# A reordered end of a loop, four copies and a root on VectorE, and an early table load, in a two-stage attention kernel

## Chip, cores and metric

One Trainium2 chip, one of its cores. The metric is the device time of one execution in microseconds (us). The kernel is written at the level of instructions: each engine has its own program, and semaphores order the engines among each other.

## What is computed

A batch of 32 sequences of 256 tokens with 256 features. A first attention with 16 heads, over batch 0 alone, is added to `x`. Then each batch goes through this, with `input_features` = `ctx` and `query_feature` = `x`:

```
norm_X   = layernorm(input_features, norm1)
norm_F_L = layernorm(query_feature, norm2)
attended = softmax(norm_F_L @ norm_X.T / 16) @ norm_X
h        = gelu(attended @ fc1_w.T + fc1_b)          # 4 hidden values per token
cross    = h @ fc2_w.T + fc2_b
nc       = layernorm(cross, norm3)
self     = softmax(nc @ nc.T / 16) @ nc
out      = norm_F_L + gamma2 * (cross + gamma1 * self)
```

Because `cross` is a linear function of 4 hidden values and a constant, the kernel never builds it at 256 features. The second attention works on rows of 6 values per token (`u`, `uK`); its layernorm needs one value per token, the variance (a quadratic form of `h`), and its reciprocal square root (`r3`).

## The kernel before

After a prologue (the first attention), the work falls into two loops.

**First loop**, 32 steps `b`, one for each batch (L1242 on TensorE, L900 on ScalarE, L540 on VectorE). `score` (L1078) makes the scores in one of three PSUM banks, `maximum` on VectorE their row maxima, `exponentials` on ScalarE the weights, `weights_turned` (L1089) turns them on TensorE, `weights_copied` on ScalarE copies them out of PSUM. Every four batches, a quad: `project` and `project_back` make values (`turned_values` and `values` copy them), `apply` and `apply_back` multiply weights and values (`applied` and `saved` copy them). The hidden values of the quads go through Gelu in three shares: `hidden(0)` at b = 21 (quads 0 to 3), `hidden(1)` at b = 29 (quads 4 and 5), `hidden(2)` in the second loop (quads 6 and 7). Gelu and Exp need different tables of ScalarE, so a Gelu among Exps costs two table loads.

**Second loop**, steps `p` = 0 to 20, one pair of batches in each of the first 16. For a pair: `turn` (L1140) turns its small rows (the operands of the scores) into PSUM bank 4, `turned` (L890, ScalarE) copies them out as `sT`, `scores` (L1162) makes the scores, `maxima` (L577, VectorE) their row maxima, `maxima_turn` (L1178) turns those into bank 5, `maxima_turned` (L923, ScalarE) copies them out as `nm2T`, `shift` (L1187) adds them to the scores, `weights` (L929, ScalarE) takes Exp. Every second step `attend` (L1198) multiplies weights and values of a quad into bank 5, `collected` copies them out as `o2T` (the tile's storage is named wqT, and so is it in the trace), `back` turns them, `returned` (VectorE) divides, `output_cuts` (GpSimd) splits into bf16 parts `sC`, `output_turn` and `output_turned` turn them, and `output` makes the result, which `finish` (L593, VectorE) adds to `Fall`, from where SyncE stores it.

Step `p` of TensorE is: `maxima_turn(p)`, `scores(p+1)`, `turn(p+2)`, `shift(p)`, then `output(p-5)`, and `attend` with `output_turn` at even p, `back` at odd p. `keep_busy(n, bank)` (L967) is n matmuls whose result nobody reads; each is two instructions in the trace.

**The algebra of shares 1 and 2** (16 tiles each) is made by GpSimd: `squares` (L744), `scaled` (L750, which ends with the power -1/2 of the variances, L758, and with `u`, L759), `keyed` (L762) and `right` (L767). VectorE then makes the left operands in `second_left` (L452, six instructions). GpSimd's order is `right(0)`, `squares(0)`, `scaled(0)`, `keyed(0)`, `right(1)`, `squares(1)`, `output_cuts(0)`, `scaled(1)`, `output_cuts(1)`, `keyed(1)`, `right(2)`, `output_cuts(2..7)`. The results of `scaled(1)`, `keyed(1)` and `right(2)` are needed by VectorE at p = 8 and by TensorE at p = 10; `output_cuts(q)` is needed by TensorE at p = 2q + 4. `newton` (L438) is one step of a reciprocal square root on VectorE, three instructions; share 0 uses it in the first loop already.

Of the kernel before, what the change touches and what calls it, by code (L numbers as in the profile page):

```python
# [72 lines left out]
def build(nc, x, ctx, x0t, c0t, wqt, wkt, wvt, params, out):  # L73
# [38 lines left out]
    minus_half = sb("minus_half", [P, 16])  # L112
    XT = sb("XT", [P, 4, DC, 2 * N])
# [127 lines left out]
    STORED = tuple(range(PAIRS))  # L241

# [50 lines left out]
    def _(dve):  # L293
# [158 lines left out]
        def second_left(h):  # L452
            G = quarter(h)
            dve.wait_ge(summed_ok, 8 * (h + 1))
            dve.wait_ge(rooted_ok, 7 * (h + 1))
# [127 lines left out]

        def returned(q):
# [18 lines left out]
        saved(QUADS - 1)  # L603
        for p in range(2 * QUADS + 5):
            if p + 1 < PAIRS:
                maxima(p + 1)
            if p % 2 == 1 and 3 <= p < 2 * QUADS + 1:
                returned((p - 3) // 2)
# [4 lines left out]
            if p == 0:  # L613
                hidden_input(2)
            if p == 2:
                second_left(0)
            if p == 8:
                second_left(1)

    @block.gpsimd  # L620
    def _(pool):
# [128 lines left out]
        def scaled(h):  # L750
# [7 lines left out]
            rooted(pool.tensor_tensor(y, var[:, G], minus_half[:, 0:GROUP // 2], ALU.pow))  # L758
# [38 lines left out]
        squares(0)  # L797
        scaled(0)
# [12 lines left out]
    def _(act):  # L811
# [88 lines left out]
        for b in range(B):  # L900
# [5 lines left out]
            if b >= 1:  # L906
                weights_copied(b - 1)
            exponentials(b)
            if b % 4 == 1 and q >= 1:
# [13 lines left out]
        def maxima_turned(p):  # L923
# [3 lines left out]
            act.activation(nm2T[:, p % 2, :], bank[5][0:2 * VW, 0:P // 2].bitcast(BF16), ACT.Copy).then_inc(m_ok, 1)  # L927
# [39 lines left out]
    def _(pe):  # L967
# [210 lines left out]
        def maxima_turn(p):  # L1178
            pe.wait_ge(max2_ok, p + 1)
            if p >= 3 and p % 2 == 1:  # L1180
# [3 lines left out]
            pe.transpose(bank[5][0:2 * VW, 0:P // 2].bitcast(BF16), nm2[:, p % 2, :, :].rearrange("p m r -> p (m r)"),  # L1184
# [57 lines left out]
        for b in range(B + 1):  # L1242
# [3 lines left out]
            if b < B:  # L1246
# [10 lines left out]
            if b == 31:  # L1257
                scores(0)
# [14 lines left out]
            if b == 31:  # L1273
                turn(1)
        for p in range(2 * QUADS + 5):
            if p < PAIRS:
                maxima_turn(p)
            if p == 0:
                keep_busy(3, 6)
                apply(QUADS - 1)  # L1280
# [4 lines left out]
            if p + 2 < PAIRS:  # L1285
                turn(p + 2)
            if p < PAIRS:
# [70 lines left out]
```

## Time and profile before

| | us |
|---|---|
| median of 3 runs | 236.84 (236.83 to 241.5) |
| the profiled execution | 236.88 |
| its span, first to last instruction | 234.8 |
| share of the span: TensorE (PE), VectorE (DVE), ScalarE (ACT), GpSimd (POOL) | 89%, 78%, 66%, 62% |
| second loop, from its first maxima turn to the end of the span | 171.2 to 234.8 |

All times in rows are microseconds from the start of the span, unless marked ns. PE is TensorE's matmul and PEld its weight load. The page adds up how long each engine was busy and cuts the span into 40 slices. The timeline lists instructions by start and duration, with the idle time in front of them and what ended it. The chain of work that ended last is followed back from the last instruction, each piece to what released it.

### The profile page before, as it was taken

To read this page: it belongs to the slowest core of one execution; us is meant where nothing else is said; L and a number is where in the kernel's file an instruction comes from. 1 tells how busy PE (TensorE), PEld (TensorE's weight loads), DVE (VectorE), ACT (ScalarE), POOL (GpSimd) and SP (SyncE) were. 2 spreads that over 40 slices of the span, in tenths; PEclk is the share of its full clock that TensorE was granted. 3 is DMA by queue.
4 is the path that set the end of the run, shared out by engine and by line. 5 is a ranking of instruction groups with operands and counts; after the bars stand their busy time and mean duration, and the time that the engine had idled before them with its cause. 6 is when DMAs were issued, how large, how long until landed. Compare 5 with 4: busy or idle time off the path is not lost.

```text
span 234.8 us, 4965 instructions
## 1 busy us (share of the span) xinstructions
PE 209.6 (89%) x1730; PEld 151.6 (65%) x1730; DVE 182.5 (78%) x360; ACT 153.8 (66%) x295; POOL 146.7 (62%) x240
## 2 busy tenths in 40 slices
PE   8999979987779999999999989997998898899760
PEld 8776646776556978789787867794766444454230
DVE  6499977779979988878778999993333867988673
ACT  2177865544546877778777896789558786677520
POOL 6536551467499999987987793934953288322320
PEclk9999999999999999999999999999999999999855
DMA  6990000084540554426535200000000004444458
GB/s 227 384 332 4 1 1 3 0 223 138 178 179 3 179 179 138 149 78 180 179 108 158 94 3 0 6 0 1 3 0 0 3 15 167 179 181 180 183 212 324
DMA packets 14712, 26.81 MB, mean 114 GB/s; under 512 B 1760, under 2 KB 1760, under 8 KB 14688
## 3 DMA queue, kind: packets, MB, share of 16 engines
q1 hardware_dynamic: 14400, 25.98, 32.3%
q10 hardware_dynamic: 288, 0.52, 0.7%
q8 instruction: 14, 0.23, 0.4%
q14 instruction: 10, 0.08, 0.1%
HBM read 18.11 MB, written 8.39 MB: 113 GB/s over the span
## 4 chain that ended last, share of the span: by engine, by line
PE 53%; DVE 20%; ACT 10%; POOL 8%; issue 6%; DVEq 0%; ACTq 0%; POOLq 0%
PE psum L1085 15%; PE psum L1022 9%; PE psum L1093 5%; DVE xN L381 4%; DVE bn L361 4%; PE psum L970 3%; PE psum L1123 3%; DVE Fall L596 2%; DVE hmax L399 2%; PE psum L1105 2%; PE psum L1205 2%; DVE nmax L523 2%; ACT L862 2%; PE psum L1238 1%; ACT E L887 1%
## 5 line engine op out<-in xcount | busy, mean ns | idle before, releaser
L1085 PE MATMUL psum<-XT,Fall 128*128 128x256 f32 x256 | 61.0, 381 | 1.7 <-ACT Fall L857 1.7
L1085 PEld LDWEIGHTS psum<-XT,Fall 128*128 128x128 f32 x256 | 46.1, 190 | 7.3 <-ACT Fall L857 2.3
L700 POOL TENSOR_SCALAR cN<-cN,nmean,rstd 128x256 f32<-128x256 f32 x64 | 37.4, 594 | 2.5 <-POOL rstd L687 2.1
L680 POOL TENSOR_TENSOR xN<-xN,tgt 128x512 f32<-128x512 f32 x28 | 35.6, 1277 | 4.8 <-DVE xN L381 4.8
L687 POOL TENSOR_TENSOR rstd<-vps,minus_half 128x8 f32<-128x8 f32 (+1 forms) x16 | 24.2, 1512 | 19.9 <-DVE vps L372 19.6
L887 ACT ACTIVATE E<-psum,nmax 128x256 f32<-128x256 f32 x64 | 26.8, 474 | 11.9 <-DVE nmax L523 11.9
L880 ACT ACTIVATE PT<-psum 128x512 f32<-128x512 f32 x32 | 19.1, 598 | 22.7 <-PE psum L1093 22.6
L523 DVE TENSOR_REDUCE nmax<-psum 128x2 f32<-128x512 f32 x32 | 22.0, 687 | 14.7 <-PE psum L1085 14.2
L381 DVE TENSOR_SCALAR xN<-xN,bn,rstd 128x256 f32<-128x256 f32 x64 | 32.8, 558 | 0.5 <-POOL rstd L687 0.4
L581 DVE TENSOR_REDUCE nm<-psum 128x4 bf16<-128x1024 f32 x16 | 19.5, 1220 | 8.2 <-PE psum L1173 8.2
L854 ACT ACTIVATE XT<-psum,b1s,w1s 128x512 f32<-128x512 f32 x32 | 23.0, 795 | 4.0 <-PE psum L1022 4.0
L857 ACT ACTIVATE Fall<-psum,par 128x512 f32<-128x512 f32 x32 | 23.4, 794 | 2.8 <-PE psum L1022 2.8
L361 DVE BATCH_NORM_STATS2 bn<-xN 128x6 f32<-128x512 f32 x32 | 21.9, 690 | 2.1 <-POOL xN L680 2.1
L361 DVE BATCH_NORM_STATS2 bn<-cN 128x6 f32<-128x512 f32 x32 | 22.2, 695 | 0.1
L1093 PE MATMUL psum<-ident,E 128*128 128x128 f32 x128 | 20.1, 280 | 1.3 <-ACT E L887 1.3
L1093 PEld LDWEIGHTS psum<-ident,E 128*128 128x128 f32 x128 | 14.4, 141 | 9.1 <-issue 6.3
L596 DVE TENSOR_TENSOR Fall<-psum,Fall 128x1024 f32<-128x1024 f32 x15 | 18.1, 1216 | 0.8 <-PE psum L1238 0.8
L1022 PE MATMUL psum<-ident,cN 128*128 128x128 f32 x128 | 17.4, 275 | 1.2 <-POOL cN L700 1.2
L970 PE MATMUL psum<-meanw 128*128 128x128 f32 x116 | 17.5, 301 | 1.0 <-POOL meanw L622 1.0
L1022 PE MATMUL psum<-ident,xN 128*128 128x128 f32 x128 | 16.9, 274 | 1.3 <-DVE xN L381 1.1
L935 ACT ACTIVATE PT<-psum 128x1024 f32<-128x1024 f32 x16 | 16.3, 1019 | 1.0 <-PE psum L1192 1.0
L970 PEld LDWEIGHTS psum<-meanw 128*128 128x128 f32 x116 | 15.6, 211 | 1.7 <-POOL meanw L622 1.0
(173 smaller groups left out, 351.9 us busy)
## 6 DMA issues: line engine op xcount, KB each, us to landing
cN<-ctx SPq DMA_DIRECT2D x32, 256.0 KB, 3.0
xN<-x SPq DMA_DIRECT2D x32, 256.0 KB, 4.1
out<-Fall SPq DMA_DIRECT2D x32, 256.0 KB, 2.3
x0T<-x0t ACTq DMA_DIRECT2D x1, 256.0 KB, 3.0
c0T<-c0t ACTq DMA_DIRECT2D x1, 256.0 KB, 3.9
wqT<-wqt SPq DMA_DIRECT2D x1, 256.0 KB, 3.6
wkT<-wkt SPq DMA_DIRECT2D x1, 256.0 KB, 4.1
wvT<-wvt SPq DMA_DIRECT2D x1, 256.0 KB, 4.8
```

The lines of the kernel that those rows point to most:

```text
L361: dve.bn_stats(bn[:, (b // 2) % 4, side, b % 2, :], src[:, b % SLOTS, :].rearrange("p (t d) -> p d t", t=NT)).then_inc(st_ok, 1)
L381: dve.tensor_scalar(own, own, stat(p, 1, m, t, 1), root_of(p, 1, m, t), ALU.subtract, ALU.mult)\
L523: dve.tensor_reduce(nmax[:, b % 2, :], tiles(bank[SBANK1[b % 3]]), AX.X, ALU.max, negate=True)\
L680: pool.tensor_tensor(xN[:, b % SLOTS, :], xN[:, b % SLOTS, :], tgt2[:, :, :].rearrange("p t d -> p (t d)"), ALU.add).then_inc(y_ok, 1)
L687: pool.tensor_tensor(rstd[:, p % 4, sides, :].rearrange("p s k -> p (s k)"), vps[:, p % 4, sides, :].rearrange("p s k -> p (s k)"), minus_ ...
L700: pool.tensor_scalar(own, own, nmean[:, p % 4, NT * m + t:NT * m + t + 1], root_of(p, 0, m, t), ALU.add, ALU.mult)\
L857: act.activation(Fall[:, 2 * p:2 * p + 2, c, :], tiles(own), ACT.Identity, bias=c_("b2", c), scale=c_("w2", c)).then_inc(evac_ok, 1)
L887: act.activation(E[:, b % 2, t * N:(t + 1) * N], bank[SBANK1[b % 3]][:, t * N:(t + 1) * N], ACT.Exp, bias=nmax[:, b % 2, t:t + 1]).then_in ...
L970: pe.matmul(bank[b][:, 0:P], meanw[:, :], meanw[:, :], start=True, stop=True)
L1022: last = pe.transpose(bank[TBANK[n % 3]][:, m * N + t * P:m * N + (t + 1) * P], z[:, (2 * p + m) % SLOTS, t * D + c * P:t * D + (c + 1) * ...
L1085: last = pe.matmul(bank[SBANK1[b % 3]][:, t * N:(t + 1) * N], Fall[:, b, c, t * P:(t + 1) * P], XT[:, p % 4, c, m * N:(m + 1) * N], start= ...
L1093: last = pe.transpose(bank[SBANK1[b % 3]][:, k * N + t * P:k * N + (t + 1) * P], E[:, b % 2, t * N + k * P:t * N + (k + 1) * P], ident[:, :])
```

## The change

It does the following; nothing else in the program differs.

1. End of the first loop. On ScalarE `turned_values(7)` goes ahead of `exponentials(29)` and `weights_copied(29)` and `(30)` go behind the exponentials of their step. On TensorE `score(31)` moves from the front of step 31 to step 30, and `scores(0)` behind `weights_turned(30)`.
2. Start of the second loop. On TensorE at p = 0, `scores(1)` and `shift(0)` go ahead of `apply(7)`, `apply_back(7)` goes to p = 1, and the fillers change from 3 + 5 + 13 to 2 + 13 + 4 calls. On ScalarE `weights(0)` goes ahead of `applied(7)`, and on VectorE `saved(7)` behind `maxima(1)` and `turned(2)`. The turned maxima of p = 3 go to bank 7, not bank 5.
3. `turned(2)` to `turned(5)` are made by VectorE.
4. `hidden(2)` (Gelu) goes behind `weights(1)`, and an Exp of one column (`warm`) follows it, so that Exp's table is loaded there.
5. For share 2, GpSimd makes the variances right behind `squares(1)`, VectorE the root (`second_root`, behind step 3: two integer instructions and three Newton steps, 11 instructions in all that each wait for the one before), and GpSimd goes on with `u`. `right(2)` comes ahead of `output_cuts(1)`.

```diff
+        def turned(p):                                   # VectorE
+            dve.wait_ge(st_mm, p + 1)
+            dve.wait_ge(s2_mm, p - 1)
+            dve.tensor_copy(sT[:, p % 2, :], bank[4][:, 0:NT * P].bitcast(BF16)).then_inc(sT_ok[p % 2], 1)
+        def second_root():
+            G = quarter(1)
+            v, y = var[:, G], r3[:, G]
+            dve.wait_ge(rooted_ok, 12)
+            link(dve.tensor_scalar(y.bitcast(I32), v.bitcast(I32), 1, None, ALU.logical_shift_right))
+            link(dve.tensor_scalar(y.bitcast(I32), y.bitcast(I32), -1.0, RSQRT_SEED, ALU.mult, ALU.add))
+            for _ in range(NEWTON - 1):
+                newton(v, y, t3[:, G])
+            newton(v, y, t3[:, G])
...
         maxima(0)
-        saved(QUADS - 1)
         for p in range(2 * QUADS + 5):
             if p + 1 < PAIRS:
                 maxima(p + 1)
+            if p < 4:
+                turned(p + 2)
...
             if p == 0:
+                saved(QUADS - 1)
                 hidden_input(2)
             if p == 2:
                 second_left(0)
+            if p == 3:
+                second_root()
...
         squares(1)                                       # GpSimd
+        variances(1)
         output_cuts(0)
         scaled(1)
+        right(2)
         output_cuts(1)
         keyed(1)
-        right(2)
...
-            if b >= 1:                                   # ScalarE, first loop
+            if 1 <= b < B - 2:
                 weights_copied(b - 1)
+            if b == B - 3:
+                turned_values(QUADS - 1)
             exponentials(b)
...
+            if b >= B - 2:
+                weights_copied(b - 1)
...
             if p == 0:                                   # ScalarE, second loop
+                weights(0)
                 applied(QUADS - 1)
+            if 4 <= p < PAIRS - 2:
+                turned(p + 2)
+            if 1 <= p < PAIRS:
+                weights(p)
             if p == 1:
                 hidden(2)
-            if p + 2 < PAIRS:
-                turned(p + 2)
-            if p < PAIRS:
-                weights(p)
+                act.activation(warm[:, :], minus_half[:, 0:1], ACT.Exp)
...
-            if b < B:                                    # TensorE, first loop
+            if b < B - 1:
                 score(b)
...
-            if b == 31:
-                scores(0)
+            if b == B - 2:
+                score(B - 1)
...
+            if p == 1:                                   # TensorE, second loop
+                apply_back(QUADS - 1)
             if p + 1 < PAIRS:
                 scores(p + 1)
             if p == 0:
-                apply_back(QUADS - 1)
...
+                shift(0)
+                apply(QUADS - 1)
+                turn(2)
+                keep_busy(2, 5)
...
+                    if p == 2:
+                        keep_busy(4, 6)
```

## Rows read from the trace of the kernel before

**Rows 1.** The page: busy time by engine, and TensorE's granted clock in 40 slices.
```profile
PE 209.6 (89%) x1730; PEld 151.6 (65%) x1730; DVE 182.5 (78%) x360; ACT 153.8 (66%) x295; POOL 146.7 (62%) x240
...
PEclk9999999999999999999999999999999999999855
```

**Rows 2.** Timeline, TensorE at the join: start, duration, engine, line, tiles, count, idle before.
```profile
164.00 0.44 PE L1113 MATMUL psum<-ident,vT 128*128 128x128 f32 x2 [1.22 <-ACT vT L868]
164.37 1.05 PE L1123 MATMUL psum<-PT,V 128*5 128x256 f32 x16
...
166.07 1.95 PE L1085 MATMUL psum<-XT,Fall 128*128 128x256 f32 x8
...
170.58 0.66 PE L1093 MATMUL psum<-ident,E 128*128 128x128 f32 x4 [0.25 <-ACT E L887]
...
177.14 3.17 PE L970 MATMUL psum<-meanw 128*128 128x128 f32 x26
180.23 0.24 PE L1184 MATMUL psum<-identb,nm 128*64 128x128 bf16 x1
```

**Rows 3.** Timeline, ScalarE: table loads of the last two Gelus.
```profile
161.54 1.28 ACT L887 ACT_TABLE_LOAD   x1
...
176.55 1.28 ACT L862 ACT_TABLE_LOAD   x1
...
178.61 1.28 ACT L935 ACT_TABLE_LOAD   x1
```

**Rows 4.** Timeline, VectorE early in the second loop: its idle time.
```profile
174.24 0.20 DVE L538 COPY OA<-psum 128x40 f32<-128x40 f32 x1 [4.26 <-PE psum L1131]
...
181.50 1.23 DVE L581 TENSOR_REDUCE nm<-psum 128x4 bf16<-128x1024 f32 x1 [3.62 <-PE psum L1173]
...
184.44 1.22 DVE L581 TENSOR_REDUCE nm<-psum 128x4 bf16<-128x1024 f32 x1
```

**Rows 5.** Timeline, GpSimd: squares of share 2, first and last instruction.
```profile
178.18 1.00 POOL L738 TENSOR_TENSOR kv<-ha,Q 128x400 f32<-128x400 f32 x1 [4.50 <-ACT ha L862]
...
180.26 0.41 POOL L748 TENSOR_TENSOR W<-kv 128x80 f32<-128x80 f32 x1
```

**Rows 6.** Chain that ended last, in order of time: start, duration, what.
```profile
182.64 0.26 DVE uK L456
...
189.56 2.93 POOL r L758
...
201.26 0.41 PE psum L1224 x4
```

**Rows 7.** Timeline, TensorE in the second loop: maxima turns (L1184) and an output turn.
```profile
189.05 0.22 PE L1184 MATMUL psum<-identb,nm 128*64 128x128 bf16 x1 [0.34 <-ACT wqT L942]
...
194.74 0.40 PE L1224 MATMUL psum<-identb,sC 128*128 128x128 bf16 x4 [0.67 <-POOL sC L794]
...
210.26 0.22 PE L1184 MATMUL psum<-identb,nm 128*64 128x128 bf16 x1
...
213.36 0.22 PE L1184 MATMUL psum<-identb,nm 128*64 128x128 bf16 x1 [0.26 <-ACT wqT L942]
...
215.90 0.22 PE L1184 MATMUL psum<-identb,nm 128*64 128x128 bf16 x1
```

**Rows 8.** Groups by line and form, VectorE: busy us, mean ns, idle before.
```profile
L405 DVE COPY PT<-psum 128x512 f32<-128x512 f32 x8 | 5.5, 683 | 0.8 <-PE psum L1051 0.8
L348 DVE TENSOR_SCALAR kv<-psum,par 128x256 f32<-128x256 f32 x4 | 1.7, 478 | 1.5 <-PE psum L990 1.5
L440 DVE SCALAR_TENSOR_TENSOR t<-t,var 128x32 f32<-128x32 f32 x3 | 0.8, 278 | 0.1
L439 DVE TENSOR_TENSOR t<-r 128x32 f32<-128x32 f32 x3 | 0.6, 191 | 0.1
```

**Rows 9.** Timeline, TensorE: the same attend (L1205) at either clock.
```profile
217.36 1.05 PE L1205 MATMUL psum<-PT,u 128*6 128x256 f32 x16
...
221.29 1.43 PE L1205 MATMUL psum<-PT,u 128*6 128x256 f32 x16 [0.63 <-DVE co L590]
```

**Rows 10.** Windows: length, busy us of PE, PEld, DVE, ACT, POOL, then PEclk, DMA, GB/s.
```profile
222.00:224.00 2.00, 2.00 (x18) 0.88 (x10) 0.35 (x2) 0.38 (x1) 0.79 (x3) 0.50 0.47 171
```

More of the change, by code:

```diff
@@ L241, in build, with maxima_bank @@
     STORED = tuple(range(PAIRS))
+    def maxima_bank(p):
+        return bank[7 if p == 3 else 5][0:2 * VW, 0:P // 2].bitcast(BF16)
     def result(n):
@@ L582, in maxima @@
                               ALU.max, negate=True).then_inc(max2_ok, 1)
+        def turned(p):
[11 more added lines that the diff above has]
+            newton(v, y, t3[:, G])
+            ALG["root"] = count[0]
         def returned(q):
@@ L748, in squares, with variances @@
             summed(pool.tensor_tensor(W5[:, G, :].unsqueeze(3), q[:, :, :, 0:1], q[:, :, :, 4:5], ALU.add))
-        def scaled(h):
+        def variances(h):
             G = quarter(h)
@@ L757, in scaled @@
             rooted(pool.tensor_scalar(var[:, G], var[:, G], EPS, None, ALU.add))
-            rooted(pool.tensor_tensor(y, var[:, G], minus_half[:, 0:GROUP // 2], ALU.pow))
+            if h == 0:
+                rooted(pool.tensor_tensor(y, var[:, G], minus_half[:, 0:PART], ALU.pow))
+        def scaled(h):
+            G = quarter(h)
+            y = r3[:, G]
+            if h == 1:
+                pool.wait_ge(alg, ALG["root"])
             rooted(pool.tensor_tensor(u[:, G, 0:H + 1], ha[:, G, :], y.unsqueeze(2).to_broadcast([P, GROUP // 2, H + 1]),
@@ L797, in _ @@
         squares(0)
+        variances(0)
         scaled(0)
@@ L926, in maxima_turned @@
                 act.wait_ge(s2m_mm, p - 1)
-            act.activation(nm2T[:, p % 2, :], bank[5][0:2 * VW, 0:P // 2].bitcast(BF16), ACT.Copy).then_inc(m_ok, 1)
+            act.activation(nm2T[:, p % 2, :], maxima_bank(p), ACT.Copy).then_inc(m_ok, 1)
         def weights(p):
@@ L1179, in maxima_turn @@
             pe.wait_ge(max2_ok, p + 1)
-            if p >= 3 and p % 2 == 1:
+            if p == 3:
+                pe.wait_ge(o_saved, QUADS)
+            elif p >= 3 and p % 2 == 1:
                 pe.wait_ge(o2T_ok, (p - 1) // 2)
@@ L1183, in maxima_turn @@
                 pe.wait_ge(co_ok, (p - 2) // 2)
-            pe.transpose(bank[5][0:2 * VW, 0:P // 2].bitcast(BF16), nm2[:, p % 2, :, :].rearrange("p m r -> p (m r)"),
+            pe.transpose(maxima_bank(p), nm2[:, p % 2, :, :].rearrange("p m r -> p (m r)"),
                          identb[:, :]).then_inc(m_mm, 1)
@@ L1272, in _ @@
                 turn(0)
-            if b == 31:
+            if b == B - 1:
+                scores(0)
                 turn(1)
@@ L1283, in _ @@
             if p == 0:
-                apply_back(QUADS - 1)
-            if p + 2 < PAIRS:
-                turn(p + 2)
-            if p < PAIRS:
-                shift(p)
-                if p < 2:
-                    keep_busy((5, 13)[p], 5)
+                shift(0)
+                apply(QUADS - 1)
+                turn(2)
+                keep_busy(2, 5)
+            else:
+                if p + 2 < PAIRS:
+                    turn(p + 2)
+                if p < PAIRS:
+                    shift(p)
+                    if p == 1:
+                        keep_busy(13, 5)
             if p == 2 * QUADS:
```

9 lines of the change are left out of this document (4 added, 5 removed).

## The prediction

> **What bounds the kernel now.** I read the page first: TensorE is busy 89% of the span and was granted full clock until the last slices [rows 1]. A share of busy time says little for the second loop, since fillers are in it, so I went on to the timelines of all engines from 157 us on, and then to the chain that ended last. Three stretches show.
>
> The join of the loops, 164 to 180 us: TensorE waits 1.22 us for the copy of the last values and once more ahead of the last turned weights [rows 2]. ScalarE loads Exp's table in front of that copy, and later pays two loads one behind the other around the third Gelu [rows 3], during which TensorE runs a filler of 26 instructions, 3.17 us [rows 2]. VectorE is idle for 4.26 and 3.62 us [rows 4].
>
> The middle, 182 to 204 us: the chain goes from VectorE (182.64) through GpSimd, with its power of 2.93 us, to the output turn at 201.26 on TensorE [rows 6]. The reader is to see that GpSimd, idle before, is late with `sC` twice, by 0.67 us [rows 7] and about as much at 201.26.
>
> The steady part: from 210.26 to 213.36 an even step takes 3.10 us, from there to 215.90 an odd one 2.54 [rows 7], a pair 5.64. VectorE needs, in a pair, two maxima and two sums of about 1.13 us pitch and a division of 0.35, so 4.9 us. It has 0.75 us to spare, not more.
>
> **The change, step by step.** I write out the new order with the durations of the rows. Each start stands beside the old one.
>
> *End of the first loop.* The copy of the last values no longer stands behind the table load, so TensorE's wait of 1.22 us goes. `score(30)` ends at 162.62 as before; from start to start `project_back` takes 0.37 (164.00 to 164.37), `apply(6)` 0.98, a `score` 1.78 of its 1.95 [rows 2], so `score(31)` is through at 165.75. `turned(0)` on ScalarE begins at 166.95 (behind `weights_copied(29)`) and `exponentials(31)` behind it, 167.45 to 168.28. TensorE's last filler there ends at 169.25, so the last weights are turned at 169.3, not 170.58 [rows 2]: 1.3 us earlier. ScalarE then copies two weights and the operand of pair 1, until 171.0; `scores(1)` goes at 171.1, `shift(0)` at 171.4, `apply(7)` to 172.7. `turn(2)` and a filler of 0.55 end at 173.5: maxima turn 1. The filler of 26 follows `shift(1)` at 174.9 and ends at 178.0: **maxima turn 2 at 178.0, old 180.23** [rows 2], 2.2 us earlier.
>
> *Gelu and its loads.* They now lie behind `weights(1)`: ScalarE ends that at 176.05, load 1.28, Gelu 0.26, load 1.28, the short Exp 0.2, free at 179.1. The first load is under the filler. The second is not quite: `shift(2)` could go at 178.6 and waits until 179.4, 0.8 us. Then `attend(0)` and the filler of 8: maxima turn 3 at 181.6. A rule speaks against this edit. The row shows a load of 1.28 us with the Gelu or Exp beginning 0.02 us behind it [rows 3]. "ScalarE: Activation LUTs" of the Trainium skill, section "What ACT_TABLE_LOAD costs", counts a drain of about 1.38 us on top, about 2.66 us a switch; the trace doesn't agree, and by that rule the sum below would lose about 1.3 us more and end at 236.6.
>
> *Copies on VectorE.* No row shows a bf16 copy of 128x512 from PSUM on VectorE. The same count in f32 takes 683 ns, half of it 478 [rows 8]; I take 0.68 (0.6 pitch) as the nearest in elements, with 0.48 as the lower bound and ScalarE's own 0.60 between. The first two are hidden in VectorE's idle time [rows 4]; `turned(4)` and `turned(5)` lie on its path. "VectorE: DVE Perf Modes" of the Trainium skill, in its section on the TRN2 errata, gives (120 + elements/acceleration) cycles at 0.96 GHz for a PSUM source, an estimate of 0.66 us at one element a cycle and 0.39 at two; no run here shows this form, and at 0.39 the sum would be some 0.5 us lower.
>
> *VectorE from 179.8 on.* `maxima(3)` ends at 179.8, `turned(4)` 0.6, `second_left(0)` 1.8 (182.64 to 184.44 [rows 4, 6]): 182.2. `scores(4)` ends at 182.2 as well, so `maxima(4)` ends at 183.4, `turned(5)` at 184.0, `returned(0)` 184.4. Here comes the root: 11 instructions with a wait each. The rows of the same code in the first loop are 191 and 278 ns for 32 columns [rows 8], the larger mean containing a disturbed one, and 0.22 us from start to start. I take 0.22, so 2.45 us; at 0.30 it is 3.3, and nothing smaller than 0.2 is in sight: 2.2. GpSimd's squares and variances are ready for it: squares took 178.18 to 180.67 [rows 5], now 177.7 to 180.2, and five small instructions more end at 181.9, while the root begins at 184.3. So this wait costs nothing; its cover is 2.4 us. The root ends at 186.8. Behind it on VectorE's queue stands `maxima(5)`, whose scores are ready at 185.4: it ends at 188.0, and with it comes **maxima turn 5 at 188.2, old 189.05** [rows 7]. Of the 2.2 us gained at the join, 0.85 is left: VectorE takes back the rest.
>
> *GpSimd afterwards.* The division of quad 0 is ready at 184.4; cuts(0) take 1.7 us, `u` then waits for the root only to 186.8, `right(2)` ends near 189.5, cuts(1) run 190.8 to 192.5, `keyed(1)` ends by 195.6. TensorE asks for cuts(1) at 193.2, so the wait of 0.67 us [rows 7] goes, and the one at 201.26 [rows 6] too. Steps 5 to 7 last 2.54 + 3.10 + 2.54 rather than 189.05 to 197.94: maxima turn 7 at 193.9, the back turn of quad 2 at 195.4, VectorE's division at 195.85, old 197.35: **1.5 us earlier**. From there VectorE is busy without a gap (finish, maxima, finish, `second_left(1)` of 1.8, maxima), as it was before, so of the second GpSimd wait nothing more can be had: the sum for that pair is 4.9 + 1.8 = 6.7 us against TensorE's 5.64. The 1.5 us pass through to the end, since steps 10 to 15 and the tail are the same.
>
> *The sum.* +2.2 (join) − 1.35 (VectorE in steps 2 to 5) + 0.7 (GpSimd's lateness) = 1.55 us, rounded 1.5. Against the profiled execution, 236.88 with 234.8 of span, that is 235.3 with a span of 233.2; the median, 236.84, is the same within 0.04. With the copy at 0.48 and the root at 2.2 it is 0.5 less, 234.8; with the root at 3.3 it is 0.85 more, 236.2. A difference within 2% (4.7 us) is about what a measurement of this kernel can tell from no change.
>
> **Rivals.**
> 1. *VectorE's root undoes all.* If each of the 11 instructions takes 0.30 us, or GpSimd's variances come behind 184.3 because Gelu is late, `maxima(5)` ends near 188.9 and maxima turn 5 is where it was; what is left is the 0.7 of GpSimd: 236.2. For it: the 278 ns row. Against it: the smaller tile, and 2.4 us of cover.
> 2. *More is had.* VectorE's copies are short, the `shift(2)` wait is nil because `maxima_turned(2)` finds ScalarE free, and the two `sC` waits with the `cT` waits behind them give their full 1.9 us: 2.2 + 1.9 − 0.5 of VectorE = 3.6 us, 233.3. Against it: VectorE has no gap from p = 7 to p = 9.
> 3. *Slower: the clock falls in the second loop.* Fillers go from 21 to 19 calls and other places; in my order TensorE idles 1.1 us ahead of `scores(1)`, 0.5 at 178.9, 0.9 at 183.2 and 0.9 ahead of maxima turn 5. In the trace the clock is full from the start until the tail, where at 222 us it is 0.50 [rows 10], 1.2 GHz, behind two gaps of 0.3 and 0.6 us and little work. There an attend takes 1.43 us rather than 1.05 although it began before the fall was complete [rows 9], and copies of four instructions grow by half. A pair of steps would be some 2.5 us longer, so from about 3.5 us of steps at the low clock on it is slower than before; two pairs give 235.3 + 5 = 240.3, one 237.8. Against it: in the old trace TensorE idled 1.22, 0.6 and 0.67 us in this region at full clock [rows 2, 7].
> 4. *No effect.* The join's gain is eaten in steps 2 to 5 and second-order waits (bank 7 of p = 3 behind `saved(7)`, `cT`) take the rest: 236.9.
>
> **How the numbers follow.** Forecast 0.50 (its own range 234.6 to 236.0), root dear 0.17 (236.2), more 0.15 (233.3, of which under 232.1 0.03), no effect 0.11 (236.9), clock 0.07 (237.8 to 240.3, above 241.6 0.01 or so). The likeliest gives 235.3. The range leaves out the clock case and the outer part of "more": 233.5 to 236.9. Faster by over 2% 0.03, within 2% 0.95, slower 0.02.
>
> **What would show it.** In the changed kernel's trace: Right for the join if the last turned weights begin near 169.3 and maxima turn 2 near 178.0; the table load behind Gelu should stand ahead of the short Exp, and `weights(2)` have none. Right for VectorE if the copies last about 0.68 us, the root 2.45, and maxima turn 5 stands near 188.2 with its wait on VectorE. Right for GpSimd if no output turn waits for `sC`. Wrong if VectorE waits for GpSimd ahead of the root, if the clock row shows less than full before slice 37, if the division of quad 2 doesn't stand 1.5 us earlier than 197.35, or if steps 10 to 15 have another length than before.

## The result

The changed kernel takes 232.99 us (median of 4 runs; 232.56 to 233.31) against 236.84, a ratio of 0.984 with a 95% interval of 0.982 to 0.986: 3.85 us less, where 1.5 were forecast, and below the range of 233.5 to 236.9. Some runs of a kernel are slower than the rest, at a lower granted clock, and the ratios leave them out (here the one of 241.5 us). The profiled execution took 233.31 with a span of 231.5.

The page of the changed kernel, busy time and granted clock in 40 slices:

```profile
PE 206.6 (89%) x1726; PEld 150.5 (65%) x1726; DVE 186.3 (80%) x375; ACT 151.8 (66%) x292; POOL 143.9 (62%) x239
...
PEclk9999999999999999999999999999999999999995
```

Beside [rows 1] VectorE works 3.8 us more in a span that is 3.3 us shorter, and the clock is low in one slice, not in three.

The timeline of TensorE in the changed kernel (start, duration, line, tiles, count, idle before and its releaser). L1226 is the maxima turn:

```profile
168.67 0.60 PE L1133 MATMUL psum<-ident,E 128*128 128x128 f32 x4
...
170.45 0.39 PE L1213 MATMUL psum<-sT 36*128 36x256 bf16 x4 [1.00 <-ACT sT L928]
...
177.52 0.24 PE L1226 MATMUL psum<-identb,nm 128*64 128x128 bf16 x1
...
178.85 0.39 PE L1234 MATMUL psum<-nm2T,sel 2*128 2x256 bf16 x4 [0.43 <-ACT nm2T L965]
...
183.52 0.94 PE L1010 MATMUL psum<-meanw 128*128 128x128 f32 x6 [0.69 <-DVE sT L592]
...
187.34 0.24 PE L1226 MATMUL psum<-identb,nm 128*64 128x128 bf16 x1 [0.43 <-DVE nm L586]
...
192.31 0.40 PE L1266 MATMUL psum<-identb,sC 128*128 128x128 bf16 x4
...
202.20 0.22 PE L1226 MATMUL psum<-identb,nm 128*64 128x128 bf16 x1 [0.85 <-DVE co L611]
...
213.48 0.22 PE L1226 MATMUL psum<-identb,nm 128*64 128x128 bf16 x1
```

The last turned weights begin at 168.67, not 170.58 [rows 2]; maxima turn 2 at 177.52, not 180.23; maxima turn 5 (187.34) waits 0.43 us for VectorE and stands 1.7 us ahead of the old 189.05 [rows 7]; the output turn at 192.31 no longer waits for GpSimd, where 0.67 us went before; turn 10 waits 0.85 us for VectorE's division.

The same execution on ScalarE, VectorE and GpSimd (three timelines):

```profile
177.14 1.28 ACT L1000 ACT_TABLE_LOAD   x1
178.44 0.20 ACT L1000 ACTIVATE warm<-minus_half 128x1 f32<-128x1 f32 x1
178.54 0.25 ACT L965 ACTIVATE nm2T<-psum 64x128 bf16<-64x128 bf16 x1
```
```profile
183.05 0.41 DVE L592 COPY sT<-psum 128x512 bf16<-128x512 bf16 x1
...
183.73 0.16 DVE L598 TENSOR_SCALAR r<-var 128x16 int32<-128x16 int32 x1
...
185.85 0.18 DVE L445 SCALAR_TENSOR_TENSOR r<-t,r 128x16 f32<-128x16 f32 x1
186.06 1.22 DVE L586 TENSOR_REDUCE nm<-psum 128x4 bf16<-128x1024 f32 x1
```
```profile
181.13 0.26 POOL L782 TENSOR_SCALAR var<-var 128x16 f32<-128x16 f32 x1
...
183.94 0.33 POOL L819 CAST sC<-co 128x160 bf16<-128x160 f32 x1 [2.55 <-DVE co L611]
...
186.10 0.32 POOL L791 TENSOR_TENSOR u<-ha,r 128x80 f32<-128x80 f32 x1 [0.32 <-DVE r L445]
```

The load is where it was meant to be: the Exp of one column begins 0.02 us behind it, and `nm2T` is copied right after. A copy lasts 0.41 us, the root 183.73 to 186.03, 2.3 us, with `maxima(5)` behind it. GpSimd has the variances at 181.39 and then idles 2.55 us: in this gap the power of 2.93 [rows 6] would nearly have fitted.

### Where the time went

Lengths between landmarks, in us, each worked out from the starts of the maxima turns in a kernel's timeline; `mt0` is maxima turn 0, "end" that of the last sum, and the stretch from `mt15` to it is called the tail. "q" is the length of the same eight matmuls of the q projection, some 5 us into the span. The kernels of the other rows are explained under Experiments.

| trace | q | mt0 at | mt0-mt2 | mt2-mt5 | mt5-mt9 | mt9-mt15 | mt15-end |
|---|---|---|---|---|---|---|---|
| before | 2.71 | 171.17 | 9.06 | 8.82 | 12.53 | 17.42 | 11.98 |
| after | 2.40 | 169.20 | 8.32 | 9.82 | 11.40 | 17.83 | 11.15 |
| join_alone | 2.75 | 169.73 | 8.32 | 8.82 | 12.53 | 19.95 | 12.02 |
| gpsimd_alone | 1.99 | 170.31 | 9.07 | 8.82 | 11.38 | 17.83 | 11.15 |
| join_gpsimd | 2.88 | 169.87 | 8.32 | 8.82 | 11.37 | 17.85 | 12.05 |
| copies_act | 2.15 | 168.94 | 8.33 | 9.65 | 11.40 | 17.84 | 11.15 |
| root_gpsimd | 1.99 | 168.53 | 8.32 | 9.73 | 11.37 | 17.84 | 11.14 |
| plain_best | 2.43 | 169.41 | 8.31 | 9.26 | 11.73 | 17.85 | 11.14 |
| no_warm | 2.74 | 169.71 | 8.32 | 9.44 | 11.27 | 18.11 | 11.14 |

From before to after: 1.97 to mt0, 0.74 to mt2, −1.00 to mt5, 1.13 to mt9, −0.41 to mt15, 0.83 in the tail, together 3.26 us, the difference of the spans (3.3).

The medians differ by 3.85, about half a microsecond more. Half of that is that the profiled run of the changed kernel lies 0.32 above its median. The other half lies outside the spans: what a run takes beyond its span is 1.8 to 1.9 us in every run of the kernels that have the Newton steps on VectorE (the changed kernel among them), 1.9 to 2.0 in root_gpsimd, and 2.1 to 2.2 in all others, before among them. So some 0.3 us of the gain goes with the root's move to VectorE, though no trace shows where.

### The profile page after: what moved, and what is told of

It is laid out like the page before. It is cut to its first block, busy times and chain, and to the rows that moved or that the text cites. A ratio compares the mean times of both kernels' runs of the same rounds, so it can differ in the third digit from the quotient of the medians.

```text
span 231.5 us, 4967 instructions
## 1 busy us (share of the span) xinstructions
PE 206.6 (89%) x1726; PEld 150.5 (65%) x1726; DVE 186.3 (80%) x375; ACT 151.8 (66%) x292; POOL 143.9 (62%) x239
## 3 DMA queue, kind: packets, MB, share of 16 engines
HBM read 18.11 MB, written 8.39 MB: 114 GB/s over the span
## 4 chain that ended last, share of the span: by engine, by line
PE 61%; DVE 21%; ACT 8%; issue 5%; POOL 2%; DVEq 0%; ACTq 0%; POOLq 0%
PE psum L1125 18%; PE psum L1062 10%; PE psum L1133 5%; PE psum L1010 4%; DVE Fall L617 4%; DVE xN L385 3%; DVE bn L365 3%; PE psum L1163 3%; PE psum L1247 3%; PE psum L1145 3%; DVE hmax L403 2%; DVE nmax L528 2%; PE psum L1280 2%; PE psum L1213 2%; PE psum L1234 2%
## 5 line engine op out<-in xcount | busy, mean ns | idle before, releaser
L1010 PE MATMUL psum<-meanw 128*128 128x128 f32 x112 | 17.0, 302 | 1.7 <-POOL meanw L647 1.0
L1010 PEld LDWEIGHTS psum<-meanw 128*128 128x128 f32 x112 | 15.1, 212 | 2.5 <-POOL meanw L647 1.0
```

Source lines behind the costliest of these rows:

```text
L1010: pe.matmul(bank[b][:, 0:P], meanw[:, :], meanw[:, :], start=True, stop=True)
```

## Experiments

Each is a small edit of the changed kernel unless it says otherwise. Times are medians with the lowest and highest of all runs. The groups of experiments ran on different chips, and mt0 moves with the prologue by up to 1.1 us between executions, so a difference of a few tenths between two medians says little. The lengths from mt0 to mt15 repeat within 0.03 us where the clock is full (47.37, 47.38 and 47.37 in three profiles of the changed kernel, 47.83 twice in before), and the argument rests on them.

### The parts alone

**join_alone** keeps items 1 and 2 and undoes 3, 4 and 5.

```diff
-            if p < 4:                                   # VectorE
-                turned(p + 2)
-            if p == 3:
-                second_root()
...
-            if 4 <= p < PAIRS - 2:                      # ScalarE
+            if p == 1:
+                hidden(2)
+            if p < PAIRS - 2:
                 turned(p + 2)
...
```

GpSimd works in its old order, with its power. On ScalarE, Gelu stands ahead of `turned(3)` and `weights(1)`, and there is no early load.

> Items 1 and 2 of the change without 3, 4 and 5: turned(2) to turned(5) and Gelu with its two loads on ScalarE where they were, the second root by GpSimd's power behind output_cuts(0). Theory (the order at the join is the largest part and nothing on VectorE was needed to keep it): maxima turn 2 at 177.5, scores(3) near 179.2 rather than 181.07, and all of steps 3 to 15 about 2 us earlier than before, GpSimd's two waits as before: 234.7. Rival (Gelu's loads in front of weights(1) eat the gain): 235.8 to 236.8. The granted clock in the tail can add or take about 1 us.

Measured 232.74, 232.86, 236.96 and 237.32 us: no run near 234.7. The two low ones are as short as the changed kernel's. The profile is of the 237.32 run, and there the clock fell in the middle. TensorE's timeline of join_alone:

```profile
178.05 0.24 PE L1217 MATMUL psum<-identb,nm 128*64 128x128 bf16 x1
178.51 0.40 PE L1204 MATMUL psum<-sT 36*128 36x256 bf16 x4 [0.22 <-ACT PT L965]
...
199.07 0.40 PE L1257 MATMUL psum<-identb,sC 128*128 128x128 bf16 x4 [0.70 <-POOL sC L818]
...
201.55 1.48 PE L1001 MATMUL psum<-meanw 128*128 128x128 f32 x6
202.96 0.32 PE L1217 MATMUL psum<-identb,nm 128*64 128x128 bf16 x1
203.21 0.61 PE L1204 MATMUL psum<-sT 36*128 36x256 bf16 x4
```

Both loads ahead of `weights(1)` lie under the filler: `scores(3)` waits 0.22 us. TensorE's waits for GpSimd are back (0.70 at 199.07), and at 201.55 the fillers take 1.48 us for the 0.83 of elsewhere. The gain of the join, 0.74 to mt2 and 1.4 at mt0 for nearly the same q (2.75 and 2.71), is held to mt5 in full (8.82, as before). The expected 234.7 lies between the two pairs of runs.

**gpsimd_alone** is the kernel before with GpSimd's order of item 5 and the power kept on GpSimd.

```diff
         squares(1)
+        variances(1)                                    # with the power
         output_cuts(0)
         scaled(1)
+        right(2)
         output_cuts(1)
         keyed(1)
-        right(2)
```

> Kernel before with GpSimd's new order alone: variances and power of share 2 right behind squares(1), right(2) ahead of output_cuts(1); nothing else. Theory: both waits of TensorE for sC (0.67 and 0.69 us) and the two waits for cT behind them (0.28 each) go, but VectorE's full stretch from p = 7 to 9 gives back a part: 0.9 to 1.4 us, 235.4 to 235.9. Rival (the waits come back elsewhere in full): 236.8.

235.5 us (234.19 to 240.23; nine of ten below 236); the interval of the ratio to before is 0.991 to 0.998. The table has 1.15 us from mt5 to mt9 and 0.41 given back behind it: 0.74 net, with nothing done on VectorE. The output turn of quad 1 has no wait (timeline of gpsimd_alone):

```profile
193.15 0.40 PE L1230 MATMUL psum<-identb,sC 128*128 128x128 bf16 x4
193.81 0.22 PE L1190 MATMUL psum<-identb,nm 128*64 128x128 bf16 x1 [0.27 <-ACT wqT L948]
```

### Was VectorE's part of the work a gain?

**copies_act** puts the four copies back on ScalarE; **root_gpsimd** makes the second root by the power, right behind the early variances; **copies_twice** makes each copy on VectorE twice; **variances_late** puts `variances(1)` behind `output_cuts(0)`.

```diff
-            if p < 4:                                   # copies_act: VectorE
-                turned(p + 2)
-            if 4 <= p < PAIRS - 2:                      # copies_act: ScalarE
+            if p < PAIRS - 2:
                 turned(p + 2)
...
-            if h == 0:                                  # root_gpsimd: GpSimd
-                rooted(pool.tensor_tensor(y, var[:, G], minus_half[:, 0:PART], ALU.pow))
+            rooted(pool.tensor_tensor(y, var[:, G], minus_half[:, 0:PART], ALU.pow))
...
-                second_root()                           # root_gpsimd: VectorE, with its if
```
```diff
+            dve.tensor_copy(sT[:, p % 2, :], ...).then_inc(twice_ok, 1)      # copies_twice
+            dve.wait_ge(twice_ok, p - 1)
             dve.tensor_copy(sT[:, p % 2, :], ...).then_inc(sT_ok[p % 2], 1)
...
-        variances(1)                                    # variances_late
         output_cuts(0)
+        variances(1)
```

> Changed kernel with turned(2) to turned(5) back on ScalarE, in front of the Exp of their step. Theory (VectorE relieves ScalarE, which is held by Gelu's loads): weights(1) and with it Gelu and both loads come 0.5 us later, weights(2) 1.0 us later, but VectorE is spared 0.33 us twice: 233.3 to 233.7. Rival (moving the copies was needless): 233.0. Second rival (VectorE is the bound in steps 2 to 5, so the move was harmful): 232.5.

232.53 us (232.44 to 232.91). The expectation named 233.3 to 233.7 and was wrong. The second rival has the time, but only 0.15 us of it is the edit's: from mt0 to mt15 it takes 47.22 us rather than 47.37, and mt0 came 0.26 earlier with a shorter q. Without the copies on VectorE TensorE has no wait ahead of maxima turn 4 (0.69 in the changed kernel), but then it waits the longer for the maxima behind the root (timeline of copies_act; 0.43 in the changed kernel):

```profile
186.92 0.24 PE L1224 MATMUL psum<-identb,nm 128*64 128x128 bf16 x1 [0.80 <-DVE nm L586]
```

> Changed kernel with the second root by the power on GpSimd right behind the early variances (181.4 to 184.3, where GpSimd is idle) and no root on VectorE. Theory (what counts is that variances and root leave the stretch behind output_cuts(0); VectorE's 2.3 us are as good as hidden because TensorE's attend sets maxima turn 5 within 0.1 us): 232.7 to 233.1. Rival (the root on VectorE was the gain): 233.8 or more, with output_cuts(0) 0.4 us late and an output turn waiting for it. Rival of the prediction (VectorE takes back the join's gain through the root): 0.5 to 0.9 us faster, 232.3.

232.91 us (232.66 to 233.28): beside the copies the root on VectorE was no gain. From mt0 to mt15 it takes 47.26 us, 0.11 less than the changed kernel. The power runs at 180.81 for 2.93 us where GpSimd is idle, and maxima turn 5 now waits for ScalarE's `o2T` and comes 0.09 us earlier behind mt0 (timelines of root_gpsimd, GpSimd and TensorE):

```profile
180.81 2.93 POOL L780 TENSOR_TENSOR r<-var,minus_half 128x16 f32<-128x16 f32 x1
183.81 0.32 POOL L813 CAST sC<-co 128x160 bf16<-128x160 f32 x1
```
```profile
186.58 0.22 PE L1220 MATMUL psum<-identb,nm 128*64 128x128 bf16 x1 [0.34 <-ACT wqT L974]
```

> Changed kernel, but each of the four VectorE copies of sT (0.41 us there, 0.33 from start to start) is made twice, the second behind a wait for the first: each takes about 0.66 us more of VectorE's queue in place of 0.33, near the 0.6 pitch that the prediction assumed. Theory (the copy's size was the mis-sized term, two of the four lie on VectorE's path to maxima(5)): maxima turn 5 at 187.9 to 188.1 rather than 187.34, about 0.6 to 0.7 us slower, 233.6. Rival (TensorE or ScalarE sets maxima turn 5 and the copies are hidden): 233.0.

234.12 us over ten runs, seven of them 233.46 to 234.32 and three 236.88 to 239.73. The seven lie 0.5 to 1.3 us above the median of the changed kernel, the lower end as expected. In the profiled one mt0 to mt4 took 15.64 us rather than 15.18, because TensorE waited 1.15 us rather than 0.69 for the second copy of `turned(5)`; then the clock fell at 185.1. So the longer copy costs through TensorE's wait for it, one step ahead of the path by `maxima(5)` that the expectation named.

> Changed kernel with share 2's variances behind output_cuts(0), where they were before; the root stays on VectorE. Theory (the wait ahead of the root is covered only because the variances are early): they end at 187.5, the root at 189.9, maxima(5) at 191.0, maxima turn 5 at 191.2 rather than 187.3, 3.5 us slower, 236.5. Rival (slack elsewhere takes it up): below 234.5.

240.28 us (240.19 to 240.74). The mechanism came as written, the price did not. TensorE's timeline of variances_late:

```profile
190.87 0.31 PE L1226 MATMUL psum<-identb,nm 128*64 128x128 bf16 x1 [3.97 <-DVE nm L586]
191.11 0.61 PE L1213 MATMUL psum<-sT 36*128 36x256 bf16 x4
...
200.79 0.38 PE L1198 MATMUL psum<-identb,sU 128*128 128x128 bf16 x4
```

Maxima turn 5 comes at 190.87 (191.2 expected) behind 3.97 us of idle time, and then four matmuls take 0.61 us, not 0.39, until 200.7: half clock for some 10 us. Of the 7.3 us above the changed kernel 3.5 are the wait and the rest the clock, which the expectation of 236.5 left out.

### The early load, and the filler

**no_warm** leaves out the Exp of one column. **plain_best** is copies_act and root_gpsimd together, with Gelu behind `weights(1)` and the early load kept. **join_gpsimd** differs from plain_best by item 4 alone: Gelu ahead of `turned(3)` and `weights(1)`, no early load. **short_filler** has `keep_busy(3, 5)` for `keep_busy(13, 5)`.

```diff
-                act.activation(warm[:, :], minus_half[:, 0:1], ACT.Exp)      # no_warm
```
```diff
+            if p == 1:                                  # join_gpsimd, against plain_best
+                hidden(2)
             if p < PAIRS - 2:
                 turned(p + 2)
             if 1 <= p < PAIRS:
                 weights(p)
-            if p == 1:
-                hidden(2)
-                act.activation(warm[:, :], minus_half[:, 0:1], ACT.Exp)
```

> Changed kernel without the Exp of one column, so that Exp's table is loaded in front of weights(2). Theory: maxima_turned(2) and shift(2) come 0.5 us earlier (no wait for ScalarE), weights(2) 0.8 us later (load 1.28 behind shift(2)), maxima turn 3 at 180.9 but scores(4) waits for weights(2) until 181.3: within 0.3 us of the changed kernel, 232.8 to 233.2. Rival (the early load is what keeps TensorE going): 233.9.

233.05 us (232.45 to 233.61), the same as with the load. Maxima turn 3 comes 0.5 us sooner behind mt2, as expected, and half of that is given back: from mt0 to mt15 it takes 47.14 us rather than 47.37. The Exp that was to put the load out of the way gained nothing.

> Changed kernel with the four copies on ScalarE and the second root by GpSimd's power behind the early variances; Gelu behind weights(1) and the early Exp table load kept. Differs from join_gpsimd by item 4 alone. Theory: VectorE is spared 3.9 us but ScalarE is held until about 179 by Gelu's loads, so shift(2) is 0.8 us late as in the changed kernel: maxima turn 0 to 15 46.9 to 47.1 us, 232.4. Rival (item 4 costs nothing): as join_gpsimd.

233.42 us (233.0 to 233.81), not 232.4, although mt0 to mt15 takes 47.15 us, little over the 46.9 to 47.1 expected. That is only 0.22 less than the changed kernel, and what a run takes beyond its span is 0.3 more. GpSimd is late here: Gelu comes late, so the power ends at 184.80, behind the division, and TensorE waits for `sC` again (timeline of plain_best):

```profile
186.66 0.40 PE L1258 MATMUL psum<-identb,sC 128*128 128x128 bf16 x4 [0.40 <-POOL sC L818]
```

> Items 1 and 2 and GpSimd's new order with the power left on GpSimd (variances and root of share 2 right behind squares(1), right(2) ahead of output_cuts(1)); no copies of sT and no root on VectorE, Gelu in front of weights(1), no early table load. Theory (items 3, 4 and the Newton steps cost about 1.0 us in steps 2 to 5: maxima turn 5 stood 17.1 us behind maxima turn 0 in join_alone and 18.1 in the changed kernel): from maxima turn 0 to 15 46.4 us rather than 47.4, 232.0. Rival (they pay for themselves, since GpSimd's new order needs the root on VectorE): 232.9 or more.

232.2 us (231.85 to 234.2). From mt0 to mt15 46.36 us, 1.01 less than the changed kernel, 0.79 less than plain_best: 0.44 of that from mt2 to mt5 and 0.36 from mt5 to mt9, where the wait for `sC` is gone. Its profile is of the 234.2 run: there an attend at 218.51 took 1.73 us and the tail 12.05, as in before.

> Changed kernel with 3 rather than 13 filler calls behind shift(1), so that TensorE idles there for up to 2.4 us. Theory A (the filler is no cost on the path since shift(2) waits for ScalarE until 178.8, and one gap of this length does not make the clock fall): 232.8 to 233.2. Theory B (the clock falls as in variances_late, where an idle time of 4.0 us at 186.9 was followed by half clock to 200.3): two to four steps at half clock, 236 to 240. Rival (the filler is on the path): 231.5 to 232.

234.78, 235.64, 242.08 and 246.31 us: all slower, by the mechanism of theory B, though none lies in its 236 to 240. TensorE's timeline of short_filler (of the 242.08 run):

```profile
179.10 0.39 PE L1234 MATMUL psum<-nm2T,sel 2*128 2x256 bf16 x4 [1.93 <-ACT nm2T L965]
...
180.40 2.08 PE L1010 MATMUL psum<-meanw 128*128 128x128 f32 x8
182.41 0.32 PE L1226 MATMUL psum<-identb,nm 128*64 128x128 bf16 x1
```

Idle for 1.93 us and, ahead of maxima turn 2, for 0.52 us in a stretch that the ten calls had filled, the engine is at half clock from 180.3 to 200.8. The filler takes no time on the path (`shift(2)` waits for ScalarE either way, until 179.10 here and 178.85 in the changed kernel) and is worth 1.8 to 13.3 us in these four runs, against the changed kernel's median.

### Fillers in the tail

```diff
+                    else:                               # p = 15
+                        pe.wait_ge(exp2_ok, PAIRS - 1)
+                        keep_busy(2, 2)
                 output_turn(QUADS - 2)
+                keep_busy(5, 0)
...
+                        if p == 2 * QUADS + 2:
+                            keep_busy(2, 0)
```

> Kernel before with fillers in the tail: 2 calls in bank 2 at p = 15, 5 in bank 0 behind output_turn(6), 2 in bank 0 behind output_turn(7), each laid where TensorE waits anyway. The tail of the profiled run of before, last attend to the end of the last sum, took 9.69 us with the clock at half from 221.8; the changed kernel's took 8.86 with the clock at half from 224.6. Theory (part of the gain is where the clock falls in the tail): clock full to the last output, tail 8.4 to 8.9, 235.8 to 236.0. Rival (the tail's length comes from its waits): 236.8 or, by the fillers' own time, 237.2.

235.24 us (234.96 to 238.22); the interval of the ratio is 0.990 to 1.002 and holds no change. The profiled run (235.1) has a tail of 11.15 us, 0.83 less than before, and full clock to 229.6. Its prologue was short as well, q 1.97, so its time alone does not settle what the fillers bring. That they hold the clock up is seen in all runs: the mean granted clock of the span is 0.992 to 0.996 in nine of the ten, and never over 0.985 in the 19 runs of before beside them.

> Changed kernel with the same fillers in the tail. Theory: the clock falls there late already, so only 0.1 to 0.5 us is left: 232.5 to 232.9, and the runs lie closer together. Rival (fillers delay the outputs): 233.4.

233.34 us (233.01 to 233.59): nothing gained, the tail is 11.15 as it was, and the mean granted clock is 0.991 to 0.996 where the changed kernel has 0.982 to 0.985.

> join_gpsimd with fillers: 5 rather than 3 calls at p = 9, where TensorE waits 0.85 us in the changed kernel, and in the tail 2, 5 and 2 calls. Theory (join_gpsimd lost up to 2 us only where the clock fell at 218.5): maxima turn 0 to 15 46.4 us, tail 11.15 in all runs, 231.8 to 232.4, and the runs lie closer together. Rival (the fillers cost what they hold): 232.5 or more.

232.56 us (232.28 to 233.17). 46.42 us from mt0 to mt15 and a tail of 11.14, no run at 234. The median is not lower than join_gpsimd's.

### What makes the times of one kernel differ

The unchanged kernel before gave, in one comparison of 13 runs, 234.81 to 234.87 three times, 236.8 to 236.93 six times, 241.42 and 241.49, and 235.85 and 237.9. The runs of 233.46 and 238.22 of copies_twice lie as far apart. So both kernels were profiled again, on another chip.

> The kernel before, unchanged, profiled again. Theory: maxima turn 0 stands near 170.2 if the q projection took 2.0 us and near 171.2 if it took 2.7; from maxima turn 0 to 15 it takes 47.8 us unless the clock falls in between (which costs over 2 us); the tail from maxima turn 15 to the last sum takes 11.15 us or, with an early fall, 12.0; the time is the sum of these: 234.8 to 237 without a fall in between. Rival (the levels have nothing to do with the clock): some other stretch has another length.

239.91 us. mt0 stands at 170.55 with q at 2.15 us; mt15 at 222.82, so 52.27 us between them rather than 47.83; tail 11.15, with the clock full to 230.9. The clock in 40 slices, and TensorE's timeline, of before_look_1:

```profile
PEclk9999999999999999999999999999999559999995
```

```profile
181.42 1.05 PE L1205 MATMUL psum<-PT,u 128*6 128x256 f32 x16
183.14 0.29 PE L1184 MATMUL psum<-identb,nm 128*64 128x128 bf16 x1 [0.67 <-ACT wqT L942]
183.36 0.61 PE L1173 MATMUL psum<-sT 36*128 36x256 bf16 x4
...
196.30 0.61 PE L1158 MATMUL psum<-identb,sU 128*128 128x128 bf16 x4
196.84 0.39 PE L1192 MATMUL psum<-nm2T,sel 2*128 2x256 bf16 x4
```

The same program, with the same two waits of 0.59 and 0.67 us in this place, is at half clock from 183.1 to 196.8, which costs 4.4 us.

> The kernel before, unchanged, a second sample, with the same expectation as before_look_1: 47.8 us from maxima turn 0 to 15, and the time by where the clock rose and fell.

236.85 us: q 2.53, mt0 at 170.97, 47.83 us to mt15, tail 12.14 with the clock down from 221.5. This is the level of 236.84. The two looks are of one program: its tail takes 11.15 us at full clock and 12.14 behind an early fall.

> The changed kernel, unchanged, profiled again. Theory: maxima turn 0 at 168.5 to 169.7 with the q projection at 2.0 to 2.7 us, 47.37 us to maxima turn 15, tail 11.15: 232.5 to 233.7. Rival: another stretch varies.

232.72 us: q 1.97, mt0 at 168.60, 47.37 us to mt15, tail 11.15.

Then the changed kernel and join_gpsimd were run on one chip.

> The changed kernel again, unchanged, on one chip with join_gpsimd_again. Theory: 47.4 us from maxima turn 0 to 15, 232.5 to 233.5 in nearly all runs, no fall of the clock in the middle of the second loop. Rival (it only had luck in its first runs): some runs near 236 to 240.

> join_gpsimd again, unchanged. Theory (items 3, 4 and the Newton steps cost 1.0 us): 46.4 us from maxima turn 0 to 15, most runs 231.8 to 232.4, some near 234 where the clock falls early in the tail; lowest run about 1 us below the lowest of after_again. Rival (no difference): both medians within 0.3 us of each other.

After: 232.85 us (232.43 to 233.48), join_gpsimd: 232.26 (231.71 to 233.65), before beside them 236.87 (236.76 to 241.52). 47.38 and 46.35 us from mt0 to mt15. Medians and lowest runs are 0.6 and 0.7 us apart, as expected in sign, though the runs overlap and their intervals (0.974 to 0.985 and 0.972 to 0.985 of before) do too. By the traces join_gpsimd is 1.0 us shorter from mt0 to mt15, and it gives 0.3 back outside the span (2.1 to 2.2 us there, 1.8 to 1.9 in the changed kernel). It needs neither the copies nor the root on VectorE, the moved Gelu or the early load.

## Why the prediction was wrong

**The bound, right.** TensorE's order at the join, ScalarE's loads, VectorE's small reserve and GpSimd's lateness are where the differences lie.

**End of the first loop, right within about 0.2 us.** Written: last turned weights at 169.3, mt2 at 178.0, 2.2 us earlier. Measured 168.67 and 177.52, 2.71 us earlier, of which 0.3 to 0.5 came from the prologue (below); that leaves 2.2 to 2.4.

**Gelu and its loads, right in the schedule.** ScalarE was to be free at 179.1 and `shift(2)` at 179.4; they came at 178.5 and 178.85. The prediction saw that `shift(2)` would wait, but did not ask what Gelu would cost in its old place. plain_best against join_gpsimd shows 0.79 us for item 4 as a whole: with Gelu ahead of `weights(1)` the filler hides both loads, and GpSimd's power is done before the division. The load again took 1.28 us with the next activation 0.02 behind it. The drain that "ScalarE: Activation LUTs" of the Trainium skill adds in its section "What ACT_TABLE_LOAD costs" is not seen here either.

**Copies, mis-sized.** 0.68 us was taken, the nearest row in elements, and 0.41 measured, below the lower bound of 0.48 from a row of half the elements. The estimate of 0.39 from "VectorE: DVE Perf Modes" of the Trainium skill, section on the TRN2 errata, at two elements a cycle, was the near one. Both copies behind `maxima(3)` were thereby 0.27 us shorter from start to start than assumed, 0.5 us in all. copies_twice, with the copies about as long as assumed, took 233.46 to 234.32 in seven of its ten runs.

**VectorE in steps 2 to 5, right sign, too dear, and by another path.** −1.35 was written, −1.00 measured, the root took 2.3 us (2.45 written), and its variances were ready 2.3 us ahead of it (2.4 written); variances_late shows that this cover is real. But the prediction put the loss on `maxima(5)` behind the root. In the traces 0.19 of it comes ahead of maxima turn 3, where TensorE waits for ScalarE, 0.72 ahead of maxima turn 4, where it waits 0.69 for the copy `turned(5)`, and 0.09 ahead of maxima turn 5. Copies and root are two paths of nearly the same length: from mt2 to mt5, taking off the root alone gives 0.09 us, the copies alone 0.17, both together (plain_best) 0.56, the rest being the late Gelu. Of the 0.56, 0.33 is lost again from mt5 to mt9, where TensorE waits for `sC`. So all of VectorE's new work costs 0.22 us from mt0 to mt15, and the other 0.79 of what join_gpsimd gains is item 4.

**GpSimd, right.** 0.7 written, 1.13 − 0.41 = 0.72 measured, the 0.41 being VectorE's full stretch that the prediction named. gpsimd_alone has 0.74 by itself.

**"The tail is the same", the step that failed.** The prediction ends with "steps 10 to 15 and the tail are the same". Steps 10 to 15 are, 14.37 us in both. The tail is not, and it is the largest part of the miss. In the profile of before the clock fell at 221.8, ahead of two outputs, and in that of after at 224.6. Windows of both, before first (length, busy us of PE, PEld, DVE, ACT, POOL, then PEclk, DMA, GB/s):

```profile
221.75:222.00 0.25, 0.25 (x8) 0.08 (x4) 0.25 (x1) 0.00 (x0) 0.20 (x1) 0.64 0.06 8
```
```profile
224.50:224.75 0.25, 0.25 (x6) 0.24 (x6) 0.25 (x1) 0.00 (x0) 0.00 (x0) 0.69 0.84 311
```

The instructions from mt15 on and their waits are the same in both until the clock falls; the tail is 0.83 us shorter. That the clock makes this difference is shown by unchanged kernels: before's own tail took 11.15 us in before_look_1 and 12.14 in before_look_2, and join_gpsimd's 12.05 and 11.15 in two profiles. [rows 9] showed the half clock and the prediction priced it, but only as something that the change might add, never as a cost that the old number already held.

Two more terms were put at nothing without a reason. One is the prologue: the q projection, untouched by the change, took 2.71 us before and 2.40 after, and mt0 moves with it. Pairs of one profile with the old join and one with the new, and nearly equal q, have mt0 1.4 us apart (2.71 and 2.75, before and join_alone) or 1.6 (2.15, before_look_1 and copies_act), where before and after have 1.97. So 0.3 to 0.5 us of that pair is no effect of the change. The other is the time outside the span, 2.1 us before and 1.8 after.

Against the forecast of 235.3 the median of 232.99 is lower by 2.3: about 0.1 at the join, 0.35 on VectorE, 0.83 in the tail, about 0.4 in the prologue, 0.3 because the profiled run lies above its median, and 0.3 outside the span. With 1.6 for the gain at mt0, the parts of the schedule itself sum to 1.6 + 0.74 − 1.00 + 1.13 − 0.41 = 2.06 us against the 1.55 written; with them alone the time would have been 234.8, inside the range. With the 0.3 outside the span they are also about what lies between the lowest run of before on any chip (234.81) and the lowest of the changed kernel (232.43): 2.38.

**The rivals.** "More is had" gave 233.3, nearest to the time, but by the wrong way: VectorE did have no gap from p = 7 to 9, and the waits did not give 1.9 us. That it came near is luck. "The clock falls" named a real mechanism, but it hit the kernel before and not the changed one. Of the 59 later runs of before 26 have a mean granted clock of 0.966 or less, as the five profiles with a fall in the middle have (0.939 to 0.965; those without have 0.972 and more). The eleven runs of the changed kernel have 0.982 to 0.985, and none took over 233.5. The mean clock is not all: two runs of before at 0.985 took 237.8 and 237.9, and no trace shows why.

**What stays open.** Why the changed kernel escapes the fall in the middle, and the early one in the tail, was not tried by itself. From the filler of 26 to maxima turn 4 TensorE's longer waits were 0.59 and 0.67 us in before, ending 2.7 us apart, and 0.43 and 0.69 in after, ending 4.7 us apart with a filler of 8 between them. In short_filler and variances_late falls came with idle times of 1.93 and 3.97 us; that the smaller difference is the cause in the kernel before is only argued. Two counts speak against it: filled_before and gpsimd_alone have the same two waits there as before, and none and one of their ten runs show so low a clock. It is also open why q differs between executions of one kernel (1.97 to 2.88 us in all profiles), since the granted clock is recorded as full there in all of them.

## What to carry to other kernels

A time that carries a low clock in one stretch is not a base for a sum: look first where the clock is low in the profile of before, and at whether the same instructions ahead of the change have the same length in both traces, and say what the median would be without. Before moving work to another engine, look for an idle gap on the engine that has it: with Gelu in its old place, making GpSimd's variances and power earlier gave all that the Newton steps on VectorE gave. Gelu's table loads were hidden under a filler in their old place, and moving them cost 0.79 us. Where two paths of nearly the same length meet, as the copies and the root did, taking off one alone shows almost nothing, so take off both. A filler on an engine that would wait anyway was worth 1.8 us and more here.

## What the runs showed of the hardware

- A VectorE copy of 128x512 bf16 from PSUM takes 0.41 us, with the next instruction 0.33 behind its start; f32 of the same count took 0.68 [rows 8]. ScalarE's copy of the same bf16 tile took 0.60.
- TensorE's granted clock can fall to 1.2 GHz in one execution and not in another of the same program, and in before_look_1 it did so behind waits of 0.59 and 0.67 us: it was low from 183.1 to 196.8 us there, and at no time before 221.4 in before_look_2. Four bf16 matmuls of 256 columns then take 0.61 us, not 0.39. It stayed low for 7 us (join_alone) to 20 us (short_filler) though the engine was busy again.
- Eleven dependent VectorE instructions on 16 columns take 2.3 us, 0.21 from start to start; GpSimd's power on the same 16 columns takes 2.93.
- The time beyond the span is 1.8 to 1.9 us in every run of the kernels with the Newton steps on VectorE and 2.1 to 2.2 us in every run of before, join_gpsimd and plain_best; the cause was not looked for.
